# First attention's latents and their weights split into fp16 high and low parts

## What is computed

```python
q = (x @ wq.T).reshape(b, s, NH, HD).transpose(0, 2, 1, 3)
k = (x @ wk_a.T @ wk_b.T).reshape(b, s, NH, HD).transpose(0, 2, 1, 3)
v = (x @ wv_a.T @ wv_b.T).reshape(b, s, NH, HD).transpose(0, 2, 1, 3)
q = _apply_decoupled_rope(q, cosf, sinf, DROPE)
k = _apply_decoupled_rope(k, cosf, sinf, DROPE)
```

## Time and profile before

| | us |
|---|---|
| median of 3 runs | 436.71 |
| lowest and highest | 433.77, 438.2 |
| profiled execution, its own time | 436.8 |
| its span in the trace | 434.9 |
| PE busy | 342.4 (79%) |
| DVE busy | 266.0 (61%) |
| ACT busy | 201.4 (46%) |
| POOL busy | 170.7 (39%) |

### The profile page before, as it was taken

How to read it: one execution, slowest core, us unless ns; L and a number is a source line. 1 busy time by engine, 2 the same in 40 slices (tenths; PEclk the granted TensorE clock), 3 DMA queues, 4 the chain that set the end, 5 groups by cost and what they waited for, 6 DMA issues and landing times. The chain is left out here.

```text
span 434.9 us, 15308 instructions
## 1 busy us (share of the span) xinstructions
PE 342.4 (79%) x6551; PEld 274.3 (63%) x6551; DVE 266.0 (61%) x541; ACT 201.4 (46%) x453; POOL 170.7 (39%) x189
## 2 busy tenths in 40 slices
PE   1999999889878787679711389999999999952187
PEld 1886747347656665568610378888888888942166
DVE  2454355534788888848779456567665676542165
ACT  1114241637966777228810246656556556530140
POOL 3870000005466566214599111455424553344300
PEclk9999999989955555559955579999999999985579
DMA  7999000008000000000000379877886877413605
GB/s 227 397 422 359 2 2 0 0 0 291 4 4 5 5 5 5 3 3 2 1 0 0 108 253 307 246 232 224 249 243 213 257 236 214 131 22 64 205 10 199
DMA packets 48516, 55.98 MB, mean 129 GB/s; under 512 B 21536, under 2 KB 45248, under 8 KB 47936
## 3 DMA queue, kind: packets, MB, share of 16 engines
q1 hardware_dynamic: 46944, 52.54, 37.4%
q0 software_dynamic: 576, 2.23, 1.6%
q10 hardware_dynamic: 928, 0.23, 0.2%
HBM read 45.02 MB, written 9.96 MB: 126 GB/s over the span
## 5 line engine op out<-in xcount | busy, mean ns | idle before, releaser
L475 POOL TENSOR_TENSOR r<-r,cst 128x1088 f32<-128x1088 f32 x16 | 33.0, 2068 | 67.7 <-DVE ring L858 64.9
L1231 PE MATMUL ps<-r 128*128 128x256 f32 x192 | 45.1, 391 | 8.8 <-DMA r<-in_x 8.8
L1231 PEld LDWEIGHTS ps<-r 128*128 128x128 f32 x192 | 37.4, 197 | 17.2 <-issue 12.3
L1331 PE MATMUL ps<-r 17*32 17x34 f32 x2048 | 29.4, 242 | 17.5 <-DVE r L921 15.3
L723 ACT ACTIVATE r<-ps 128x504 f16<-128x504 f32 (+1 forms) x50 | 32.0, 666 | 23.2 <-PE ps L1422 22.6
L1331 PEld LDWEIGHTS ps<-r 17*32 17x32 f32 x2048 | 26.6, 141 | 25.1 <-DVE r L921 22.4
L530 POOL COPY r<-r 64x476 f16<-64x476 f16 x20 | 11.6, 580 | 74.2 <-ACT r L743 72.5
L653 ACT ACTIVATE r<-r,cst 128x136 f32<-128x136 f32 x128 | 39.9, 401 | 0.0
L548 POOL TENSOR_TENSOR r<-r,quad 128x476 f16<-128x476 f16 x40 | 38.9, 1008 | 0.0
L1422 PE MATMUL ps<-pairs_of,r 128*128 128x56 f16 x680 | 29.0, 193 | 8.7 <-DVE r L1099 4.3
L1444 PE MATMUL ps<-r,ring 128*128 128x68 f16 x840 | 35.6, 199 | 0.0
(11 more groups left out here) (157 smaller groups left out, 765.7 us busy)
## 6 DMA issues: line engine op xcount, KB each, us to landing
ring<-wsplit SPq DMA_DIRECT2D x140, 192.0 KB, 3.2
r<-in_x SPq DMA_DIRECT2D x3, 1536.0 KB, 15.8
padded_rows<-r SPq DMA_DIRECT2D x38, 112.0 KB, 3.2
r<-in_w SPq DMA_DIRECT2D x4, 768.0 KB, 12.3
wsplit<-ring SPq DMA_DIRECT2D x1, 3072.0 KB, 11.6
r<-in_x SPq DMA_DIRECT2D x4, 384.0 KB, 8.2
h<-in_pos SPq DMA_DIRECT2D x1, 1536.0 KB, 11.9
out<-h SPq DMA_DIRECT2D x3, 512.0 KB, 2.6
```

Source lines behind the costliest of these rows:

```text
L475: pool.tensor_tensor(free(kx[:, u % 2, 0, :], (ROWH, UI), (NTOK, HH), (1, NTOK)), free(kr[:, 0, UI * NTOK * u:], (NTOK, UI), (0, HH), (1, ...
L1231: mm = pe.matmul(bank((n - 1) % 2, 0, D), xT[:, c, k, i * P:(i + 1) * P], tokw[:, k, :], start=k == 0, stop=k == PKT - 1)
L1331: mm = pe.matmul(bank(4 + 2 * (u % 2) + j // 2, at, at + 2 * NTOK)[QROW * c:QROW * c + QROW], v1[rows, UG * u + g, lo:lo + QROW], p1T[rows ...
```

## The change

The latents are held as fp16 pairs. `keyl` and `vall` take the place of `lat`, each over half of its memory: in `keyl` rows 0 to 63 hold the high parts of the key latents and rows 64 to 127 their low parts; in `vall` rows 64 to 127 hold the high parts of the value latents and rows 0 to 63 the low parts. The weights are scaled and split in the same way into `wk16` and `wv16`, with the high part copied to the other 64 rows, and one fp32 matmul (two passes) becomes two fp16 ones (high weights against both parts; low weights). Columns are still read at a step of `QROW` = 32 elements, which is 64 bytes where it was 128. Scale factors are taken out in the copies from PSUM.

- `latents_out` on ScalarE makes four instructions of 64 rows in place of two of 128, and VectorE gets `latents_low`, four subtractions from PSUM for each chunk. `turn` waits for all four, `keys` for the first two.
- `latent_weights` on ScalarE and VectorE stands in pass c = 1 after the latents: two copies, two subtractions, two copies, behind `rotated` 4 and `ld["late"]`.
- `keys(0)` waits for `wl_twice` 2; the value projection waits for the last `lat_low` in place of `ld["late"]`.
- GpSimd scales `wlat` between the rotation of `wq` and that of `wk`; the first latents wait for it.
- `split_low(3)` on VectorE moves from after the last keys into pass 5, ahead of the copy of the queries.

```diff
@@ gpsimd
             for k in range(KT):
                 rotate(wq[:, k], k)
+            pool.wait_ge(ld["wlat"], 16)
+            pool.tensor_scalar(flat(wlat), flat(wlat), XS, None, ALU.mult).then_inc(rotated, 1)
             pool.wait_ge(ld["wk"], 16)
             rotate(wk, KT)
@@ scalar: project_out and v1_out get scale=1 / (XS * WS), queries 1.0
@@ scalar
             def latents_out(c):
                 chunk = CHUNKS[c]
                 act.wait_ge(lat_in, c + 1)
-                for g in range(UG):
-
-                    nc.scalar.activation(
-                        free(lat[:, chunk[0] + P * g:], (1, len(chunk)), (QROW * UI, NU), (QROW, IPG)),
-                        free(bank(2, g), (P, len(chunk)), (UI, NU), (UG, IPG)), ACT.Copy).then_inc(lat_ready, 1)
+                for rows, held in ((slice(0, 64), keyl), (slice(64, P), vall)):
+                    for g in range(UG):
+                        nc.scalar.activation(
+                            free(held[rows, chunk[0] + P * g:], (1, len(chunk)), (QROW * UI, NU), (QROW, IPG)),
+                            free(bank(2, g)[rows], (P, len(chunk)), (UI, NU), (UG, IPG)), ACT.Copy)\
+                            .then_inc(lat_ready, 1)
+
+            def latent_weights():
+
+                act.wait_ge(rotated, 4)
+                act.wait_ge(ld["late"], LATE)
+                nc.scalar.activation(wk16[:, 0, :], wk[:, 0, :], ACT.Copy, scale=WS).then_inc(wl_high, 1)
+                nc.scalar.activation(wv16[:, 0, :], wv[:, :], ACT.Copy, scale=WS).then_inc(wl_high, 1)
+                act.wait_ge(wl_low, 2)
+                nc.scalar.activation(wk16[64:P, 0, :], wk16[0:64, 0, :], ACT.Copy).then_inc(wl_twice, 1)
+                nc.scalar.activation(wv16[0:64, 0, :], wv16[64:P, 0, :], ACT.Copy).then_inc(wl_twice, 1)
@@
                 project_out(4 * (c - 1))
                 latents_out(c - 1)
+                if c == 1:
+                    latent_weights()
@@ vector: project_out and v_out become tensor_scalar with the same factors
@@ vector
+            def latents_low(c):
+                chunk = CHUNKS[c]
+                for i, (rows, held, low) in enumerate(((slice(0, 64), keyl, slice(64, P)),
+                                                       (slice(64, P), vall, slice(0, 64)))):
+                    dve.wait_ge(lat_ready, 2 * UG * c + UG * (i + 1))
+                    for g in range(UG):
+                        at = (1, len(chunk)), (QROW * UI, NU), (QROW, IPG)
+                        dve.tensor_tensor(
+                            free(held[low, chunk[0] + P * g:], *at),
+                            free(bank(2, g)[rows], (P, len(chunk)), (UI, NU), (UG, IPG)),
+                            free(held[rows, chunk[0] + P * g:], *at), ALU.subtract).then_inc(lat_low, 1)
+
+            def latent_weights():
+
+                dve.wait_ge(wl_high, 2)
+                dve.scalar_tensor_tensor(out=wk16[:, 1, :], in0=wk[:, 0, :], scalar=WS, in1=wk16[:, 0, :],
+                                         op0=ALU.mult, op1=ALU.subtract).then_inc(wl_low, 1)
+                dve.scalar_tensor_tensor(out=wv16[:, 1, :], in0=wv[:, :], scalar=WS, in1=wv16[:, 0, :],
+                                         op0=ALU.mult, op1=ALU.subtract).then_inc(wl_low, 1)
@@
+                if c == len(CHUNKS):
+                    split_low(3)
                 project_out(4 * (c - 1) + 1)
+                latents_low(c - 1)
+                if c == 1:
+                    latent_weights()
@@
             project_out(4 * (len(CHUNKS) - 1) + 3)
-            split_low(3)
@@ tensor, turn
                 if c >= 1 and k == 0:
-                    pe.wait_ge(lat_ready, UG * c)
+                    pe.wait_ge(lat_low, 2 * UG * c)
@@ tensor
             def keys(c):
                 if c == 0:
-                    pe.wait_ge(rotated, 3)
-                pe.wait_ge(lat_ready, UG * (c + 1))
-                latents = lambda k: free(lat[:, CHUNKS[c][0]:], (1, len(CHUNKS[c])), (QROW, B))
-                project(4 * c + 2, latents, lambda k: wk[:, 0, :], 1)
-                project(4 * c + 3, latents, lambda k: wk[:, 0, :], 1)
+                    pe.wait_ge(wl_twice, 2)
+                pe.wait_ge(lat_low, 2 * UG * c + UG)
+                latents = free(keyl[:, CHUNKS[c][0]:], (1, len(CHUNKS[c])), (QROW, B))
+                for f in range(2):
+                    project(4 * c + 2 + f, [(wk16[:, x, :], latents) for x in range(2)])
@@ tensor, values
-            pe.wait_ge(ld["late"], LATE)
+            pe.wait_ge(lat_low, 2 * UG * len(CHUNKS))
@@
-                    mm = pe.matmul(bank(4 + r % 4, D * i, D * i + D), lat[:, P * g:P * g + P], wv[:, :],
-                                   start=True, stop=True)
+                    for x in range(2):
+                        mm = pe.matmul(bank(4 + r % 4, D * i, D * i + D), vall[:, P * g:P * g + P], wv16[:, x, :],
+                                       start=x == 0, stop=x == 1)
```

More of the change, by code:

```diff
@@ L157, in build @@
         wv = sb("wv", D)
+        wk16 = sb("wk16", 2 * D, F16)[:, :].rearrange("p (x d) -> p x d", x=2)
+        wv16 = sb("wv16", 2 * D, F16)[:, :].rearrange("p (x d) -> p x d", x=2)
         wo1 = sb("wo1", KT * D)[:, :].rearrange("p (k d) -> p k d", k=KT)
@@ L220, in build @@
         lat_ready = sem("lat_ready")
+        lat_low = sem("lat_low")
+        wl_high = sem("wl_high")
+        wl_twice = sem("wl_twice")
+        wl_low = sem("wl_low")
         v_in = sem("v_in")
@@ L589, in project_out @@
                 nc.scalar.activation(free((qr if r % 4 < 2 else kr)[:, r % 2, chunk[0]:], (1, len(chunk)), (NTOK, B)),
-                                     free(bank(4 + r % 4), (P, len(chunk)), (1, P)), ACT.Copy).then_inc(proj_act, 1)
+                                     free(bank(4 + r % 4), (P, len(chunk)), (1, P)), ACT.Copy,
+                                     scale=1.0 if r % 4 < 2 else 1 / (XS * WS)).then_inc(proj_act, 1)
             act.wait_ge(ld["cst"], 16)
@@ L642, in v1_out @@
                 act.wait_ge(v_in, r + 1)
-                nc.scalar.activation(free(v1[:, 2 * r, :], (1, BANK)), bank(4 + r % 4), ACT.Copy).then_inc(v_act, 1)
+                nc.scalar.activation(free(v1[:, 2 * r, :], (1, BANK)), bank(4 + r % 4), ACT.Copy,
+                                     scale=1 / (XS * WS)).then_inc(v_act, 1)
             def expand(u):
@@ L850, in project_out @@
                 chunk = CHUNKS[r // 4]
-                dve.tensor_copy(free((qr if r % 4 < 2 else kr)[:, r % 2, chunk[0]:], (1, len(chunk)), (NTOK, B)),
-                                free(bank(4 + r % 4), (P, len(chunk)), (1, P))).then_inc(proj_dve, 1)
+                dve.tensor_scalar(free((qr if r % 4 < 2 else kr)[:, r % 2, chunk[0]:], (1, len(chunk)), (NTOK, B)),
+                                  free(bank(4 + r % 4), (P, len(chunk)), (1, P)),
+                                  1.0 if r % 4 < 2 else 1 / (XS * WS), None, ALU.mult).then_inc(proj_dve, 1)
+            def latents_low(c):
[15 more added lines that the diff above has]
+                                         op0=ALU.mult, op1=ALU.subtract).then_inc(wl_low, 1)
             def split_low(s):
@@ L892, in v_out @@
                 dve.wait_ge(v_in, r + 1)
-                dve.tensor_copy(free(v1[:, 2 * r, :], (1, BANK)), bank(4 + r % 4)).then_inc(v_dve, 1)
+                dve.tensor_scalar(free(v1[:, 2 * r, :], (1, BANK)), bank(4 + r % 4), 1 / (XS * WS), None, ALU.mult)\
+                    .then_inc(v_dve, 1)
             dve.wait_ge(w_low, 4)
@@ L1246, in turn, with project @@
                 mm.then_inc(xn_turned, 1)
-            def project(r, moving, weights, kts):
+            def project(r, terms):
                 if r >= 4:
@@ L1252, in project @@
                 n = P * len(CHUNKS[r // 4])
-                for k in range(kts):
-                    mm = pe.matmul(bank(4 + r % 4, 0, n), weights(k)[:, P * (r % 2):P * (r % 2) + P], moving(k),
-                                   start=k == 0, stop=k == kts - 1)
+                for m, (weights, moving) in enumerate(terms):
+                    mm = pe.matmul(bank(4 + r % 4, 0, n), weights[:, P * (r % 2):P * (r % 2) + P], moving,
+                                   start=m == 0, stop=m == len(terms) - 1)
                 mm.then_inc(proj_in, 1)
@@ L1263, in q_and_latents @@
                 tokens = lambda k: xnT[:, c % 2, k, 0:n]
-                project(4 * c, tokens, lambda k: wq[:, k, 0, :], KT)
-                project(4 * c + 1, tokens, lambda k: wq[:, k, 0, :], KT)
+                for f in range(2):
+                    project(4 * c + f, [(wq[:, k, 0, :], tokens(k)) for k in range(KT)])
                 if c == 0:
-                    pe.wait_ge(ld["wlat"], 16)
+                    pe.wait_ge(rotated, 3)
                 for k in range(KT):
```

2 lines of the change are left out of this document (added).

## The result

The changed kernel takes 467.23 us (464.01 to 470.32) against 436.71: 7.0% slower, ratio 1.0703, 95% interval 1.0644 to 1.0762. Slower was forecast, 445.0 us, but the time lies 16 us above the range. The profiled execution took 464.33 us, with a span of 462.5 in place of 434.9: +27.6 where the sum said +8.2. The median is +30.5. Medians count every execution; ratios leave out those that lie more than 1.5% above the fastest of their kernel.

A forecast was written before the change was run, and what follows sets the result against it. TensorE, without a hole from 9 to 80 us, was taken as the bound, then ScalarE in the value projection. The terms +14.2 +2.0 -0.4 -3.4 +0.8 -2.5 -2.5 gave +8.2, so 445.0 us, range 439.5 to 451.

The forecast's parts named there:

- The hole: Before key projection 0: TensorE stops while ScalarE waits for the late loads, then six small instructions split weights; +14.2 us.
- The half clock after it: Dense TensorE work after the stop before keys 0 runs at 1.2 GHz for a while; +2.0 us.
- I take the same factor of two: Key matmuls: fp16 at the step costs 0.436 us a pass of 512 columns, bounds 0.218 and 0.86.
- R2: Rival: in the key matmuls the fp16 step costs what it costs in fp32, 3.42 us; 451 us, chance 0.08.
- -3.4: Keys of chunks 1 and 2, in the dense stretch: 1.74 us each in place of 3.42; -3.4 us.
- R1: Rival: the stop before keys 0 stays and all gains are at their best; 439.5 us, chance 0.15.
- a pitch of 0.53: Split latents: each ScalarE copy from PSUM priced at 0.53 us, taken from two copies lasting 1.03 to 1.06.
- T+3.3: Split latents: value low parts ready 3.3 us after T, the end of the latents' matmuls.
- The cover that I named: Chunks 1 and 2: one embedding of 2.6 us before the key matmuls hides the key latents' T+2.2.
- the last but one chunk: Chunk step c = 5, with no embedding left to hide anything: queries start at T+6.3, not T+5.5; +0.8 us.
- the gate: Last chunk: both engines go on after VectorE's copy of the keys, at T+5.0 in place of T+7.5; -2.5 us.
- The value projection: After the gate: fp16 matmuls are shorter but ScalarE is the bound; -2.5 us, bounds -0.8 and -3.0.

The follow-up runs named there:

- e1: Changed kernel, with wv loaded right behind wk under its own semaphore and the weights' split waiting for that, not all late loads: 457.81 us, ratio 1.0461.
- e2: Kernel before with the wait alone: ScalarE waits for the five late loads and keys of chunk 0 wait for ScalarE: 450.43 us, ratio 1.029.
- e7: Changed kernel, with value weights split in pass c = 3 and key weights alone in pass 1, without the late-load wait: 456.17 us, ratio 1.0424.
- m1: Kernel of its own, computing nothing of the reference: times single ScalarE, VectorE and TensorE operations by type and step; no total time given.
- e6: As e9, and value latents written with a chunk's four positions innermost, in runs of four: 428.78 us; again 427.32, ratio 0.9818.
- e9: As e7, and fp16 key latents laid out by position, written in runs of four and read without a step: 437.44 us, ratio 0.9985.
- e11: The kernel of e6 run again, for an interval: 427.32 us, ratio 0.9818 to the kernel before.
- e10: The kernel of e6, with GpSimd's zero fills waiting until the heads are chosen: 419.74 us, ratio 0.9627.

## Why the prediction was right or wrong

**The hole: right.** Place, cause and size hold. `bo` landed at 36.4 us, ScalarE's first `wk16` copy began at 36.54, and keys 0 came 12.4 us late against the start of the kernel's own work, forecast 14.2 (1.5 us of the difference is a later start in this execution, which the loads don't share). e1, e2 and e7 each show it alone. The half clock after it was +1.2 for +2.0.

**"No row shows fp16 at a step of 64 bytes ... I take the same factor of two": wrong, at the bound.** The row in hand said that the step costs 0.43 us on top of 0.43. I read that as a factor; it was a floor, 0.86 us for 512 columns whatever the type. R2 had this, with a chance of 0.08 and 451 us. It moves -3.4 to 0 and takes 1.7 us each from chunks 3 and 4. (The 2.6 us that I gave for a free step are 3.0 by the terms of R1.) The Trainium skill, page "SBUF — State Buffer", section "Door 1: The DMA port swizzle (why `[64,N]` ≈ `[32,N]`)", states a penalty for each access that goes to a new line of 16 bytes. The runs agree that there is one, and it is a factor of 3.7 on the 0.24 us of contiguous fp16, not the two that I had from fp32. By the same section of the Trainium skill a step of up to 8 bf16 elements, which have two bytes as those of fp16, costs nothing. This does not hold here: at a step of 4, with two fp16 elements to a line, a pass took 0.47 us for 0.24 (m1, L161 and L157), and at a step of 8 0.92 (L163).

**"A ScalarE copy of this pattern lasts 0.63 us ... a pitch of 0.53", "so I take 0.5": the step that failed.** The pattern was the same and the type was not. No row of before writes two-byte elements at a wide step, and I took the fp32 row as the price without bounds, while I gave the matmul two. At 1.2 us for each of eight instructions the latents are ready at T+7.7, not T+3.3. The cover that I named, one embedding of 2.6 us, is then too short: stops of 2.33 us in each dense chunk, with half clock after them, +7.9 where I had 0; +7.0 for +0.8 in the last but one chunk, and 1.1 of half clock in the queries behind; +2.1 for -2.5 at the gate. Together, and without the 1.7 us that the step of the keys takes in each of the last two chunks, that is 16 us; the sum missed 19. The sentence "if that cover were gone it would cost up to 3.3 us a chunk" had the mechanism, but with a latency of 3.3 us where 7.7 was measured, and no rival was built on it.

**The value projection: right.** -1.8 for -2.5, with ScalarE as the bound: from 131.13 to 148 us it waited for TensorE once, for 0.22 us.

**The clock.** I gave its loss to the one long hole. But it fell three times more in the projections: 6.73 and 6.83 us for two embeddings of 5.36, behind stops of 2.33 us, and 4.73 for queries of 3.6, behind one of 7.42. The stops of 2.33 us alone do not explain it. In the changed kernel the granted clock was 1.00 all through the stop, from 57.4 to 59.9 us, and fell to 0.50 at about 63 us, in the fp16 keys behind it. In e1 a stop of 2.39 us before the short keys of chunk 0 cost nothing, with 5.36 us for the two embeddings behind. And m1 lost the clock behind stepped fp16 matmuls with no stop at all. How much belongs to the stops and how much to the fp16 keys at a step is open.

**"Slower" and its chance: right, for part of the reason.** The rivals on both sides were about the hole and the matmul. None had the path over ScalarE and VectorE as the new bound. The prediction also called itself wrong if a stage behind 130 us took another time than before, and so it did: the attention +1.1 us, the routing -4.9. The last was luck, and without it the profiled execution would have missed the sum by 24 us and not by 19.

## What to carry to other kernels

An instruction whose element type changes has a new price even when its pattern stays: bound it like an unknown, or lay the data out so that neither writes nor reads have a wide step. When a layout is kept from an older type, ask who still needs it; here the keys did not, and the values only needed their loop turned. A cover that hides 2.2 us of latency should be priced at two and three times that latency before it is called nothing.

## What the runs showed of the hardware

Two-byte results at a wide step cost 2.3 to 2.4 times four-byte ones on ScalarE and on VectorE (pitch 1.15 to 0.48 us and 1.15 to 0.5 us for 256 elements), and runs of four elements take the penalty away (0.30 and 0.35). For TensorE's moving operand, the tokens or latents that stream through, the distance of a column from the last sets the price from 8 bytes on: 0.46 to 0.47 us for 512 columns at 8 bytes, 0.87 to 0.94 at 16 and more, in fp16 as in fp32.

The changed kernel's routing was 4.9 us shorter than before, and nothing in it was edited. Of this 4.5 us are one small VectorE instruction, before and after:

```profile
221.15 6.01 DVE L1028 TENSOR_SCALAR r<-r 128x16 f32<-128x16 f32 x1
```
```profile
252.56 1.50 DVE L1079 TENSOR_SCALAR r<-r 128x16 f32<-128x16 f32 x1
```

GpSimd fills gaps with zeros at that time. Before, its last fill ended with the instruction (timeline of GpSimd):

```profile
226.69 0.45 POOL L512 MEMSET r<- 128x420 f32 x1
```

In the profiled executions of e1 and e7 it is short as well (1.50 and 1.29 us), in those of e2, e6, e9 and e11 it lasts 6.0 to 6.2 us; what decides was not found. So I let GpSimd wait until the heads are chosen, in the kernel before (e8) and on top of both layouts (e10):

```diff
             pool.wait_ge(wo1_done, NTOK)
+            pool.wait_ge(mask_ready, 1)
             for u in range(2):
```

> The kernel before with one wait more: GpSimd fills its gaps with zeros only after VectorE has found the chosen heads, not during it. In the profile of before one VectorE instruction of 128x16 elements there lasts 6.0 us and ends with GpSimd's fills; in the changed kernel the same instruction lasts 1.5 us, which is why the routing is 6.7 us shorter there. Theory (VectorE is held while GpSimd fills): the instruction lasts 0.2 us, the routing to the chosen heads is 5 to 8 us shorter, and the time falls by up to as much, unless GpSimd's later work becomes the bound. Rival (the long instruction has another cause): it stays at 6 or 1.5 us and nothing changes, or the time rises by GpSimd's delay.

> Both layouts and the later value weights (as e6_both_layouts, 428.8 us), and GpSimd's zero fills after the chosen heads (as e8_pool_after_mask, 6 us off the kernel before). The two gains lie in stages that only follow each other, so they should add: 422 to 424 us, 0.965 of before. If the 6 us come from an accident of phase that the earlier arrival changes, 425 to 429.

Timeline of VectorE, e8:

```profile
222.78 0.23 DVE L1029 TENSOR_SCALAR r<-r 128x16 f32<-128x16 f32 x1
```

It takes 0.23 us. But e8's six executions lie in two groups, 427.4 to 428.6 and 434.7 to 435.9 us, with a median of 431.67. The ratio of 0.9771 (0.973 to 0.9812) is that of the lower group. The profiled execution is in the upper one, at 435.94 us, and there another instruction, which took 0.46 us before, is held:

```profile
230.14 5.00 DVE L1056 TENSOR_SCALAR r<-cst,r 128x140 f32<-128x140 f32 x1
```

The first held instruction of before started 1.6 us later here (222.78 for 221.15) and was 5.8 us shorter, but the first gather began at 242.27 us for 242.56. So 1.9 us were gained of 5.8: the wait moved the hold and did not remove it. That the lower group is the executions without a hold is likely and not shown.

Each held instruction ends within 0.1 us of the end of one of GpSimd's fills: at 227.16 us and the fill at 227.14 before, where it sat through the fills up to the last; at 254.06 and 254.03 in the changed kernel, where it got in between two; at 235.14 and 235.05 in e8. So VectorE's TENSOR_SCALAR was held by the fills. Not all of VectorE is: four TENSOR_TENSOR of 128x256 elements ran under the fills of the changed kernel in 0.42 to 0.43 us each from 254.10 on. Before, beside GpSimd's additions (L516), the same four took 0.83 to 0.91.

e10 takes 419.74 us, ratio 0.9627 (0.9556 to 0.9697), 2 us below its forecast of 422 to 424 and 7.6 below e11, which ran beside it. So the two gains add up in the medians, and it is the fastest kernel of the study, 17 us under the kernel before and 47 under the changed one. In its profiled execution, its fastest (417.06), no instruction there lasts over 1.4 us; the others, up to 426.96, have no profile. Why the fills hold one instruction and not the other was not tried.
